# A selective-scan kernel on one core: work of the dt stage spread over other engines, and the outputs of both scan directions summed in PSUM

## Chip, core and metric

The kernel runs on one core of one Trainium2 chip. The metric is the device time of one execution in microseconds (us), lower is better. The engines are called as the profile calls them: PE (TensorE), with its weight loads apart as PEld, DVE (VectorE), ACT (ScalarE), POOL (GpSimd) and SP (SyncE, which issues all DMAs here).

## What is computed

Sixteen images of 56x56 tokens with 192 channels go through a windowed attention block with an MLP, and then through a two-dimensional selective scan:

```python
# layer 0: shifted window attention and MLP on x (16, 56, 56, 192)
...
# layer 1
xs = _cross_scan(xc)                      # rows, columns, and both reversed: K_DIRS = 4
x_dbl = jnp.einsum('bkdl,kcd->bkcl', xs, x_proj_weight)
dts, Bs, Cs = jnp.split(x_dbl, [R_RANK, R_RANK + N_STATE], axis=2)
dts = jnp.einsum('bkrl,kdr->bkdl', dts, dt_projs_weight)
dts = jax.nn.softplus(dts + dt_projs_bias[None, :, :, None])
A = -jnp.exp(A_logs).reshape(K_DIRS, d, N_STATE)
ys = _selective_scan(xs, dts, A, Bs, Cs)  # h = exp(dt*A)*h + dt*x*B ; y = sum_n h*C
ys = ys + Ds.reshape(1, K_DIRS, d, 1) * xs
y = _cross_merge(ys, h, w)                # all four directions added, the column ones transposed
y = layernorm over the channels
```

## The kernel before

The program has four parts, one behind the other, each with its own semaphores, and DRAM scratch tensors between them. Everything is float32 but where bf16 is named.

**Layer 0** (`build_layer0`) is not touched.

**The dt stage** (`build_prep`, called prep here) makes, for each image, the time steps dt, the products u = dt*x, and B and C. An image is cut into 4 chunks of 784 tokens (`CT`). A chunk has 7 items for PE (`PER`): six raw tiles of 128x784, of which tiles 0 to 2 belong to the row order (o = 0) and tiles 3 to 5 to the column order (o = 1, where `order` hands PE the tokens with a stride of 56), and a seventh with the raw B and C, called bc here. There are 16 x 4 = 64 chunks and 384 tiles. A raw tile goes into one of three PSUM slots of two banks; a fourth, `l_ps`, holds the logarithm. Softplus is computed in a form that is safe for large values:

- ACT makes r = relu(-raw - bias + 20) (L731), e = exp(20 - r) (L735) and l = log(1 + e) in PSUM (L720, `logs`). Behind the sixth tile of a chunk it copies bc to `bc_o` (L741).
- DVE makes m = e(e - 2) (L765, `quad`, one tile ahead), p = max(-m/2, l) in PSUM (L775), q = min(p, e) into `m_t` (L777), and dt = max(raw + bias, q) into `dt_o` (L788). The last reads the raw tile, so that its slot is free for PE only then (`free`, L669, waits for `dt_done`).
- POOL multiplies dt by x (L826) into `u_o`, and at the end of a chunk splits bc in one block (`split`, L797) into three bf16 parts (L805, L807, L809, L811).
- SP stores, in this order for each chunk: dt and u of o = 0, dt and u of o = 1, bc, and behind `low_done`, the end of the split, four stores of the parts (L638). At an image's first chunk the eight loads of the next image (L617, L619) stand ahead of the stores. `dt_o` and `u_o` have one buffer for each o, so L788 of tile 0 waits until the store of the chunk before has landed (`dt_out`).

**The scan** (`build_scan`) works through 16 units for each image (2 orders x 4 chunks x 2 directions d), each of 24 steps, 6144 steps in all. In a step DVE runs one scan instruction (L1071) and, in 18 of 24, one multiply (L1051) of u with B, which PE has spread over the partitions in PSUM (L951, `spread`, two steps ahead, one PSUM buffer). POOL multiplies the states by C (L1107) and makes the other six products with B (L1096). PE sums over the states (L960, `reduce`, six steps behind) into PSUM, and ACT evacuates a third of a unit at a time into `y_sb` (L1004). SP stores each unit's y to `scr_y`, which has a place for each order and direction. In column order the y's are in column order too.

**The output part** (`build_output`) loads, for each image and half of the channels (a = 0, 1), four y's and x; POOL adds the two directions of the column order (L1206), DVE those of the row order (L1228), DVE adds the columns to the rows through a transposed view (L1232) and the residual (L1237, `yf`). Then PE transposes, DVE takes statistics (L1244, L1250) and normalises (L1258) seven groups, and POOL applies weight and bias to each (L1211, L1213). POOL's queue is in order: the adds of the next image stand behind the last L1213 of this one.

The few lines that set the order in prep's end of a tile:

```python
dve.wait_ge(q_done, n + 1)
if j % 3 == 0:
    after(dve, dt_out[o], 16 * g)
    after(dve, u_done, TILES * (g - 1) + 3 * o + 3)
nc.vector.scalar_tensor_tensor(dt_o[:, o, j % 3], slot(PER * c + j), bpos[...], m, ALU.add, ALU.max)
```

## Time and profile before

| | us |
|---|---|
| median of 3 runs (lowest, highest) | 23655.29 (23637.66, 23655.61) |
| the profiled execution | 23647.01 |
| its span | 23645.2 |
| PE busy, share | 18035.3 (76%) |
| DVE busy, share | 19747.9 (84%) |
| ACT busy, share | 9462.4 (40%) |
| POOL busy, share | 16017.7 (68%) |
| mean granted TensorE clock | 0.738 |

The page draws the span in 40 equal slices, with each engine's busy share in tenths and the TensorE clock that was granted (a share of 0.50 is 1.2 GHz, 1.00 is 2.4 GHz; a figure between them is a mean over time spent at both). Layer 0 takes nine slices, prep four, the scan some 25 and the output part two. A matmul's end is modelled, so PE's busy time says less than the distance from one start to the next.

### The profile page before, as it was taken

To read this page: it belongs to the slowest core of one execution; us is meant where nothing else is said; L and a number is where in the kernel's file an instruction comes from. 1 tells how busy PE (TensorE), PEld (TensorE's weight loads), DVE (VectorE), ACT (ScalarE), POOL (GpSimd) and SP (SyncE) were. 2 spreads that over 40 slices of the span, in tenths; PEclk is the share of its full clock that TensorE was granted. 3 is DMA by queue.
4 is the path that set the end of the run, shared out by engine and by line. 5 is a ranking of instruction groups with operands and counts; after the bars stand their busy time and mean duration, and the time that the engine had idled before them with its cause. 6 is when DMAs were issued, how large, how long until landed. Compare 5 with 4: busy or idle time off the path is not lost. (4 is left out here: it accounts for less than half of the span.)

```text
span 23645.2 us, 289556 instructions
## 1 busy us (share of the span) xinstructions
PE 18035.3 (76%) x82840; PEld 6320.8 (27%) x82840; DVE 19747.9 (84%) x21684; ACT 9462.4 (40%) x14504; POOL 16017.7 (68%) x8708
## 2 busy tenths in 40 slices
PE   8999999997888677777777777777777777777711
PEld 5555565552222111111111111111111111111111
DVE  4555545446666899999999999999999999999977
ACT  3333333334444344444444444444444444444400
POOL 0000000004444899999999999999999999999956
PEclk9999999998888666666666666666666666666655
DMA  0000000004554656556655655655665565565588
GB/s 17 15 14 14 14 15 14 14 14 173 183 186 174 134 122 127 125 121 127 127 122 125 127 123 123 126 126 121 126 127 122 124 127 124 121 128 125 110 202 191
DMA packets 977931, 2571.14 MB, mean 109 GB/s; under 512 B 65622, under 2 KB 324056, under 8 KB 955296
## 3 DMA queue, kind: packets, MB, share of 16 engines
q1 hardware_dynamic: 976800, 2559.04, 47.2%
q8 instruction: 346, 5.67, 0.1%
q14 instruction: 785, 6.43, 0.1%
HBM read 1974.33 MB, written 584.45 MB: 108 GB/s over the span
## 5 line engine op out<-in xcount | busy, mean ns | idle before, releaser
L1107 POOL TENSOR_TENSOR c_pr<-c_hs,c_c_u 128x784 f32<-128x784 f32 x6144 | 11218.2, 1848 | 760.6 <-DVE c_hs L1071 760.6
L1014 ACT ACTIVATE c_psum<-c_dt_u,c_a_neg 128x784 f32<-128x784 f32 x6144 | 5642.0, 918 | 8506.9 <-DVE c_hs L1071 8462.4
L960 PE MATMUL c_psum<-c_pr,c_red 128*64 128x392 f32 x24576 | 8085.5, 779 | 0.9 <-POOL c_pr L1107 0.9
L1071 DVE TENSOR_TENSOR_SCAN c_hs<-c_psum,c_carry,c_dbx 128x784 f32<-128x784 f32 x3456 | 6273.1, 1846 | 0.0
L951 PE MATMUL c_psum<-c_br_u,c_sel 48*128 48x512 bf16 (+1 forms) x9216 | 3373.8, 461 | 3703.3 <-DVE c_dbx L1051 3626.2
L1051 DVE TENSOR_TENSOR c_dbx<-c_u_u,c_psum 128x784 f32<-128x784 f32 x4608 | 4391.4, 953 | 51.6 <-PE c_psum L951 51.6
L177 POOL TENSOR_TENSOR a_xpb<-a_x_sb,a_pb_sb 98x768 f32<-98x768 f32 x128 | 231.1, 1806 | 5070.5 <-DVE a_x L262 5057.0
L960 PEld LDWEIGHTS c_psum<-c_pr,c_red 128*64 128x64 f32 x24576 | 1924.0, 192 | 3748.4 <-issue 2031.7
L1096 POOL TENSOR_TENSOR c_dbp<-c_u_u,c_bp_u 128x784 f32<-128x784 f32 x1536 | 2849.7, 1855 | 39.8 <-DMA c_c_u<-scr_bc 39.8
L951 PEld LDWEIGHTS c_psum<-c_br_u,c_sel 48*128 48x128 bf16 x9216 | 565.3, 103 | 8504.1 <-DVE c_dbx L1051 8009.1
L1071 DVE TENSOR_TENSOR_SCAN c_hs<-c_psum,c_carry,c_dbp 128x784 f32<-128x784 f32 x1152 | 2133.5, 1852 | 0.0
L1071 DVE TENSOR_TENSOR_SCAN c_hs<-c_psum,c_dbx 128x784 f32<-128x784 f32 x1152 | 2019.4, 1782 | 19.7 <-issue 18.4
L826 POOL TENSOR_TENSOR p_u_o<-p_dt_o,p_xm 128x784 f32<-128x784 f32 x384 | 788.2, 2054 | 1276.6 <-DVE p_dt_o L788 1276.6
L689 PE MATMUL p_psum<-p_xm,p_wk 128*128 128x392 f32 x1536 | 985.6, 775 | 386.3 <-DVE p_dt_o L788 376.6
L407 PE MATMUL a_psum<-a_g_sb,a_w_sb 128*96 128x392 f32 x3072 | 1165.4, 502 | 0.7 <-ACT a_g_sb L306 0.7
L765 DVE SCALAR_TENSOR_TENSOR p_m_t<-p_e_t 128x784 f32<-128x784 f32 x384 | 459.3, 1196 | 779.5 <-ACT p_e_t L735 779.4
L213 DVE TENSOR_REDUCE a_mx<-a_psum 128x6 f32<-128x294 f32 x512 | 234.3, 458 | 1028.0 <-PE a_psum L422 1028.0
L398 PE MATMUL a_psum<-a_h2T,a_w_sb 96*128 96x392 f32 x3072 | 1044.4, 496 | 20.6 <-DVE a_v_sb L242 17.0
L1302 PE MATMUL d_psum<-d_id_sb,d_yf 96*112 96x96 f32 x896 | 152.1, 358 | 1009.2 <-DVE d_yf L1237 935.1
L436 PE MATMUL a_psum<-a_xnT,a_wqkv_sb 96*96 96x392 f32 x2048 | 747.9, 507 | 91.0 <-ACT a_qkT L336 88.6
L254 DVE COPY a_pT<-a_psum 49x384 f32<-49x384 f32 x512 | 280.5, 548 | 617.0 <-PE a_psum L471 617.0
L306 ACT ACTIVATE a_g_sb<-a_psum,a_b_sb 128x392 f32<-128x392 f32 x768 | 451.0, 587 | 765.5 <-PE a_psum L398 765.5
(105 smaller groups left out, 17490.3 us busy)
## 6 DMA issues: line engine op xcount, KB each, us to landing
c_c_u<-scr_bc SPq DMA_DIRECT2D x512, 1568.0 KB, 26.6
c_dt_u<-scr_dt SPq DMA_DIRECT2D x512, 588.0 KB, 7.3
c_u_u<-scr_u SPq DMA_DIRECT2D x512, 588.0 KB, 10.8
c_bp_u<-scr_bc SPq DMA_DIRECT2D x512, 392.0 KB, 20.2
scr_dt<-p_dt_o SPq DMA_DIRECT2D x128, 1176.0 KB, 4.5
scr_u<-p_u_o SPq DMA_DIRECT2D x128, 1176.0 KB, 5.6
scr_y<-c_y_sb SPq DMA_DIRECT2D x512, 294.0 KB, 14.4
d_yin<-scr_y SPq DMA_DIRECT2D x64, 2352.0 KB, 25.9
```

The source lines that it names most:

```text
L398: mm = pe.matmul(ps[:, 6 + m % 2, 0:UT], w1_sb[:, a, 128 * m:128 * m + 128], h2T[:, a, :], start=(a == 0), stop=(a == 1))
L407: pe.matmul(ps[0:HC, 6 + a, 0:UT], w2_sb[:, m, HC * a:HC * a + HC], g_sb[:, m, :], start=(m == 0), stop=False)
L436: mm = pe.matmul(ps[0:HC, 6 + e % 2, 0:UT], wqkv_sb[:, a, HC * e:HC * e + HC], xnT[:, a, :, 0:WT], start=(a == 0), stop=(a == 1))
L689: pe.matmul(bank(k, h), wk[:, o, 0, m0:m0 + 128], order(xm[:, par, 0, :], o, c, h, HT), start=True, stop=False)
L826: nc.gpsimd.tensor_tensor(u, dt, order(xm[:, par, k, :], o, c, 0, CT), ALU.mult).then_inc(u_done, 1)
L951: mm = pe.matmul(b_ps[:, n0:n1], sel[:, s % NPR, :], br_u[:, d, n0:n1], start=True, stop=True)
L960: mm = pe.matmul(Y(3 * w + q)[64 * h:64 * h + 64, :], red[:], pr[:, s % RP, HT * h:HT * h + HT], start=(p == 0), stop=(p == NPR - 1))
L1014: nc.scalar.activation(dA(s), dt_u[:, d, s // NPR, :], ACT.Exp, scale=a_neg[:, k, s:s + 1]).then_inc(exp_done, 1)
L1051: nc.vector.tensor_tensor(dbx[:, (MULS * w + i) % RB, :], u_u[:, d, s // NPR, :], b_ps, ALU.mult).then_inc(mul_done, 1)
L1071: nc.vector.tensor_tensor_scan(hs[:, s % RH, way], dA(s)[:, way], data, init, ALU.mult, ALU.add).then_inc(scan_done, 1)
L1096: nc.gpsimd.tensor_tensor(dbp[:, (len(POOL_STEPS) * w + i) % RG, :], u_u[:, d, s // NPR, :], bp_u[:, d, POOL_PAIRS.index(s % NPR), :], ALU ...
L1107: nc.gpsimd.tensor_tensor(pr[:, s % RP, :], hs[:, s % RH, :], c_u[:, d, s % NPR, :], ALU.mult).then_inc(prod_done, 1)
```

## The change

In **prep** ACT no longer makes relu; it copies the raw tile with the bias to SBUF (`lift` into `xb`, four buffers), which frees the PSUM slot; POOL clamps it to 20 (`clamp`); ACT takes exp (`grow`) and log (`logs`). The raw tiles have two slots in place of three, the logarithms two in place of one. ACT lifts two tiles ahead and grows one ahead. DVE computes max and min in place in PSUM and the last max from `xb`. POOL clamps two tiles ahead, multiplies by x one tile late, and does the split of a chunk in four pieces behind tiles 1 to 4 of the next chunk. SP's own order is not changed.

In the **scan** the two directions that cover a chunk are summed in PSUM: the unit that comes first ("opens") evacuates to `y_sb[:, cc]` and isn't stored; in the second, PE first multiplies `y_sb` by the identity into the PSUM group (`same`) and the reductions are added to that. Only the second is stored, half as many bytes.

In the **output part** two y's are loaded in place of four, and POOL does the one add that is left, rows plus transposed columns, in place; DVE's two adds are gone.

```diff
-    SLOT = [k % 3 for k in range(PER_IMG - 1)] + [1]
+    PER_CHUNK = TILES * PAIRS
...
-        slot = lambda k: ps[:, SLOT[k], :].rearrange("p (h z) -> p h z", h=2)[:, :, 0:HT]
-        l_ps = ps[:, 3, :].rearrange("p (h z) -> p h z", h=2)[:, :, 0:HT]
+        slot = lambda k: ps[:, k % 2, :].rearrange("p (h z) -> p h z", h=2)[:, :, 0:HT]
+        l_ps = lambda j: ps[:, 2 + j % 2, :].rearrange("p (h z) -> p h z", h=2)[:, :, 0:HT]
...
+        xb = sb("xb", [128, 4, 2, HT])
+        cap = sb("cap", [128, 2, 2, HT])
...
             def free(b, k):
...
+                img, j = (0, k - 2) if k >= 2 else (-1, k - 2 + PER_IMG)
                 if j % PER < TILES:
-                    after(pe, dt_done, TILES * (PAIRS * (b + img) + j // PER) + j % PER + 1)
+                    after(pe, xb_done, TILES * (PAIRS * (b + img) + j // PER) + j % PER + 1)
...
+            def lift(b, c, j):
...
+                act.wait_ge(raw_full, PER * g + j + 1)
+                after(act, dt_done, n - 3)
+                after(act, cap_done, n - 3)
+                nc.scalar.activation(xb[:, n_of(c, j) % 4], slot(PER * c + j), ACT.Identity,
+                                     bias=bpos[:, j // 3, j % 3:j % 3 + 1]).then_inc(xb_done, 1)
+                if j == TILES - 1:
                     act.wait_ge(raw_full, PER * g + PER)
...
                     nc.scalar.activation(bc_o[:, c % 2], slot(PER * c + TILES), ACT.Copy).then_inc(bc_done, 1)
+            def grow(b, c, j):
...
+                act.wait_ge(cap_done, n + 1)
+                after(act, q_done, n - 2)
+                nc.scalar.activation(e_t[:, j % 3], cap[:, j % 2], ACT.Exp).then_inc(e_done, 1)
+            def logs(b, c, j):
...
+                act.wait_ge(e_done, n + 1)
+                after(act, dt_done, n - 1)
+                nc.scalar.activation(l_ps(j), e_t[:, j % 3], ACT.Ln, bias=one[:, 0:1]).then_inc(l_done, 1)
+            def body(b, par, last):
+                for n in range(PER_CHUNK):
+                    for piece, ahead in ((lift, 2), (grow, 1)):
+                        at = step(b, n + ahead, last)
+                        if at:
+                            piece(*at)
+                    logs(*step(b, n, last))
...
-                        nc.vector.scalar_tensor_tensor(l_ps, m, -0.5, l_ps, ALU.mult, ALU.max).then_inc(p_done, 1)
+                        nc.vector.scalar_tensor_tensor(l, m_t[:, j % 2], -0.5, l, ALU.mult, ALU.max).then_inc(p_done, 1)
...
-                        nc.vector.tensor_tensor(m, l_ps, e_t[:, j % 3], ALU.min).then_inc(q_done, 1)
+                        nc.vector.tensor_tensor(l, l, e_t[:, j % 3], ALU.min).then_inc(q_done, 1)
...
-                        nc.vector.scalar_tensor_tensor(dt_o[:, o, j % 3], slot(PER * c + j), bpos[:, o, j % 3:j % 3 + 1], m,
-                                                       ALU.add, ALU.max).then_inc(dt_done, 1)
+                        nc.vector.tensor_tensor(dt_o[:, o, j % 3], xb[:, n_of(c, j) % 4], l, ALU.max).then_inc(dt_done, 1)
...
+            def clamp(b, c, j):
+
+                n = TILES * (PAIRS * b + c) + j
+                after(pool, e_done, n - 1)
+                hold(pool, xb_done, n + 1, fence)
+                nc.gpsimd.tensor_scalar(cap[:, j % 2], xb[:, n_of(c, j) % 4], CLAMP, None, ALU.min).then_inc(cap_done, 1)
...
+                        at = step(b, n + 2, last)
+                        if at:
+                            clamp(*at)
+                        if j >= 1:
+                            times_x(b, par, c, j - 1)
+                        elif c:
+                            times_x(b, par, c - 1, TILES - 1)
...
+                        if j in (1, 2, 3, 4):
+                            if c:
+                                split(b, c - 1, j - 1)
+                            elif not (isinstance(b, int) and b == 0):
+                                split(b - 1, PAIRS - 1, j - 1)
...
+        y_sb = sb("y_sb", [128, NCHK, 3, HT])
...
+        def opens(w):
+
+            return w % (2 * NCHK) < NCHK
...
+                if opens(w):
+                    return
                 hold(sp, y_evac, 3 * v + 3, fence)
...
                 if p == 0:
                     after(pe, y_evac, 3 * v + q - 1)
+                    if not opens(w):
+                        pe.matmul(Y(3 * w + q), same[:], y_sb[:, unit_of(w)[1], q, :], start=True, stop=False)
                 pe.wait_ge(prod_done, STEPS * v + s + 1)
...
-                                   start=(p == 0), stop=(p == NPR - 1))
+                                   start=(p == 0 and opens(w)), stop=(p == NPR - 1))
...
+                    rows = yin[:, a, 0].rearrange("p (h w) -> p h w", h=IMG)
+                    nc.gpsimd.tensor_tensor(rows, rows, yin[:, a, 1].rearrange("p (w h) -> p h w", h=IMG),
+                                            ALU.add).then_inc(add_done, 1)
...
-                    nc.vector.tensor_tensor(yin[:, a, 0], yin[:, a, 0], yin[:, a, 1], ALU.add).then_inc(row_done, 1)
...
-                    nc.vector.tensor_tensor(sq(yin[:, a, 0], "p (h w) -> p h w"), sq(yin[:, a, 0], "p (h w) -> p h w"),
-                                            sq(yin[:, a, 2], "p (w h) -> p h w"), ALU.add).then_inc(add_done, 1)
```

How the instructions move: POOL in prep, one chunk before (`p_u_o` is u, `p_parts` the bf16 parts):

```order
L826 TENSOR_TENSOR p_u_o<-p_dt_o,p_xm 128x784 x6
L805 CAST p_parts<-p_bc_o 128x784
L807 TENSOR_TENSOR p_rem<-p_bc_o,p_parts 128x784
L809 CAST p_parts<-p_rem 128x784
L811 TENSOR_TENSOR p_parts<-p_rem,p_parts 128x784
```

and the stretch of the changed kernel in which the split of a chunk is done, tiles 1 to 4 of the next chunk (`p_cap` is the clamped tile):

```order
L813 TENSOR_SCALAR p_cap<-p_xb 128x784
L825 TENSOR_TENSOR p_u_o<-p_dt_o,p_xm 128x784
L835 CAST p_parts<-p_bc_o 128x784
L813 TENSOR_SCALAR p_cap<-p_xb 128x784
L825 TENSOR_TENSOR p_u_o<-p_dt_o,p_xm 128x784
L839 TENSOR_TENSOR p_rem<-p_bc_o,p_parts 128x784
L813 TENSOR_SCALAR p_cap<-p_xb 128x784
L825 TENSOR_TENSOR p_u_o<-p_dt_o,p_xm 128x784
L842 CAST p_parts<-p_rem 128x784
L813 TENSOR_SCALAR p_cap<-p_xb 128x784
L825 TENSOR_TENSOR p_u_o<-p_dt_o,p_xm 128x784
L845 TENSOR_TENSOR p_parts<-p_rem,p_parts 128x784
```

The split's last piece now stands behind the multiplication of tile 3 of the next chunk.

DVE at the start of an image in the output part, before:

```order
L1228 TENSOR_TENSOR d_yin<-d_yin 96x3136
L1232 TENSOR_TENSOR d_yin<-d_yin 96x3136
L1237 SCALAR_TENSOR_TENSOR d_yf<-d_x_in,d_dsum,d_yin 96x3136
L1228 TENSOR_TENSOR d_yin<-d_yin 96x3136
L1232 TENSOR_TENSOR d_yin<-d_yin 96x3136
L1237 SCALAR_TENSOR_TENSOR d_yf<-d_x_in,d_dsum,d_yin 96x3136
L1244 BN_STATS d_stats<-d_psum 112x6 x4
```

and in the changed kernel:

```order
L1285 SCALAR_TENSOR_TENSOR d_yf<-d_x_in,d_dsum,d_yin 96x3136 x2
L1292 BN_STATS d_stats<-d_psum 112x6 x4
L1298 BN_AGGR d_mv<-d_stats 112x2 x4
L1292 BN_STATS d_stats<-d_psum 112x6 x4
L1298 BN_AGGR d_mv<-d_stats 112x2 x4
```

Four adds are gone from DVE; POOL's queue has two large adds for an image, as before.

## Rows read from the trace of the kernel before

**Rows 1.** Prep, scan: length; busy us of PE, PEld, DVE, ACT, POOL; PEclk, DMA share, GB/s.

```profile
5376.00:7730.00 2354.00, 1895.78 (x4120) 507.15 (x4120) 1533.78 (x1549) 1116.13 (x1217) 1126.16 (x640) 0.87 0.52 183
...
7770.00:22466.00 14696.00, 11036.03 (x33790) 2489.12 (x33790) 14669.29 (x10751) 6211.01 (x8958) 13931.45 (x7679) 0.65 0.59 124
```

**Rows 2.** Instructions of tile dt_o: ns least/median/most, first and last start.

```profile
L826 POOL TENSOR_TENSOR p_u_o<-p_dt_o,p_xm x384: 1841/2227/2593, 5404.6 to 7718.3; 128x784 f32<-128x784 f32 x192
```

**Rows 3.** Who waited for whom in prep: us in total, times, longest.

```profile
ACT p_bc_o L741 <- PE p_psum L701: 290.6, 64, 7.7
```

**Rows 4.** PE in prep in order of time: start, length, line, operands.

```profile
6210.29 3.13 PE L689 MATMUL p_psum<-p_xm,p_wk 128*128 128x392 f32 x4
...
6214.97 1.64 PE L698 MATMUL p_psum<-p_xm,p_wk 128*64 128x392 f32 x4
...
6221.25 1.58 PE L689 MATMUL p_psum<-p_xm,p_wk 128*128 128x392 f32 x4
...
6223.20 0.49 PE L691 MATMUL p_psum<-p_xm,p_wk 64*128 64x392 f32 x1
...
6227.89 2.98 PE L689 MATMUL p_psum<-p_xm,p_wk 128*128 128x392 f32 x4 [4.20 <-DVE p_dt_o L788]
```

**Rows 5.** Short stretches of the same time, columns as in rows 1.

```profile
6209.50:6211.40 1.90, 1.90 (x6) 0.51 (x3) 1.84 (x2) 0.96 (x2) 1.84 (x1) 1.00 0.42 170
...
6228.50:6230.40 1.90, 1.90 (x4) 0.67 (x2) 1.20 (x2) 0.00 (x0) 1.90 (x2) 0.50 0.77 307
```

**Rows 6.** Costliest groups, shapes apart: busy us, mean ns, idle time before and its releaser.

```profile
L765 DVE SCALAR_TENSOR_TENSOR p_m_t<-p_e_t 128x784 f32<-128x784 f32 x384 | 459.3, 1196 | 779.5 <-ACT p_e_t L735 779.4
L777 DVE TENSOR_TENSOR p_m_t<-p_psum,p_e_t 128x784 f32<-128x784 f32 x384 | 374.2, 975 | 13.1
L807 POOL TENSOR_TENSOR p_rem<-p_bc_o,p_parts 128x784 f32<-128x784 f32 x64 | 109.3, 1708 | 5.1
L805 POOL CAST p_parts<-p_bc_o 128x784 bf16<-128x784 f32 x64 | 60.3, 943 | 2.4 <-ACT p_bc_o L741 2.4
```

**Rows 7.** DVE in order of time, L765 while POOL was at work.

```profile
6234.46 1.81 DVE L765 SCALAR_TENSOR_TENSOR p_m_t<-p_e_t 128x784 f32<-128x784 f32 x1 [4.72 <-ACT p_e_t L735]
```

**Rows 8.** SP's queue at an image's first chunk: start, length, DMAs.

```profile
5988.39 1.84 SPq L638 DMA_DIRECT2D scr_bp<-p_parts  x4
...
5995.86 0.41 SPq L627 DMA_DIRECT2D scr_dt<-p_dt_o  x1
```

**Rows 9.** DMAs issued from 5990 to 6000: count, KB, median us to landing.

```profile
scr_dt<-p_dt_o SPq DMA_DIRECT2D x1, 1176.0 KB, 15.6
```

**Rows 10.** The same over all of prep.

```profile
scr_dt<-p_dt_o SPq DMA_DIRECT2D x128, 1176.0 KB, 4.5
```

**Rows 11.** All engines in the scan in order of time.

```profile
12000.48 1.57 PE L960 MATMUL c_psum<-c_pr,c_red 128*64 128x392 f32 x4
...
12005.51 0.83 PE L951 MATMUL c_psum<-c_br_u,c_sel 48*128 48x512 bf16 x2 [1.25 <-DVE c_dbx L1051]
```

**Rows 12.** POOL in the output part in order of time, first image.

```profile
22527.10 10.02 POOL L1206 TENSOR_TENSOR d_yin<-d_yin 96x3136 f32<-96x3136 f32 x1 [20.05 <-DMA d_x_in<-scr_x]
22553.23 1.80 POOL L1211 TENSOR_TENSOR d_ob<-d_ob,d_w_sb 112x768 f32<-112x768 f32 x1 [16.12 <-DVE d_ob L1258]
```

**Rows 13.** All engines, from the sixth image's last group to the seventh's first.

```profile
22925.90 4.98 POOL L1211 TENSOR_TENSOR d_ob<-d_ob,d_w_sb 112x768 f32<-112x768 f32 x1
...
22936.36 6.78 POOL L1206 TENSOR_TENSOR d_yin<-d_yin 96x3136 f32<-96x3136 f32 x1
...
22944.10 11.77 POOL L1206 TENSOR_TENSOR d_yin<-d_yin 96x3136 f32<-96x3136 f32 x1 [0.96 <-DMA d_x_in<-scr_x]
...
22962.51 5.96 DVE L1232 TENSOR_TENSOR d_yin<-d_yin 96x3136 f32<-96x3136 f32 x1
22968.51 3.48 DVE L1237 SCALAR_TENSOR_TENSOR d_yf<-d_x_in,d_dsum,d_yin 96x3136 f32<-96x3136 f32 x1
...
22978.53 1.80 POOL L1211 TENSOR_TENSOR d_ob<-d_ob,d_w_sb 112x768 f32<-112x768 f32 x1 [22.67 <-DVE d_ob L1258]
```

More of the change, by code:

```diff
@@ L795, in _, with times_x @@
         def _(pool):
-            def split(b, c):
+            def clamp(b, c, j):
+                n = TILES * (PAIRS * b + c) + j
+                after(pool, e_done, n - 1)
+                hold(pool, xb_done, n + 1, fence)
+                nc.gpsimd.tensor_scalar(cap[:, j % 2], xb[:, n_of(c, j) % 4], CLAMP, None, ALU.min).then_inc(cap_done, 1)
+            def times_x(b, par, c, j):
+                g, o, k = PAIRS * b + c, j // 3, j % 3
+                pool.wait_ge(dt_done, TILES * g + j + 1)
+                if k == 0:
+                    after(pool, u_out[o], 16 * g)
+                dt = dt_o[:, o, k].rearrange("p h t -> p (h t)")
+                u = u_o[:, o, k, :]
+                if o:
+                    dt, u = (a.rearrange("p (w r) -> p w r", r=IMG) for a in (dt, u))
+                nc.gpsimd.tensor_tensor(u, dt, order(xm[:, par, k, :], o, c, 0, CT), ALU.mult).then_inc(u_done, 1)
@@ L815, in body @@
                 for c in range(PAIRS):
[L816 removed]
                     for j in range(TILES):
[L818 to L827 removed]
+                        n = n_of(c, j)
+                        at = step(b, n + 2, last)
+                        if at:
+                            clamp(*at)
[4 more added lines that the diff above has]
+                        elif not (isinstance(b, int) and b == 0):
+                            times_x(b - 1, 1 - par, PAIRS - 1, TILES - 1)
+                        if j in (1, 2, 3, 4):
+                            if c:
+                                split(b, c - 1, j - 1)
+                            elif not (isinstance(b, int) and b == 0):
+                                split(b - 1, PAIRS - 1, j - 1)
+                if last:
+                    times_x(b, par, PAIRS - 1, TILES - 1)
+                    for part in range(4):
+                        split(b, PAIRS - 1, part)
+            clamp(0, 0, 0)
+            clamp(0, 0, 1)
             halves(pool, body)
 def build_scan(nc, io, dts, us, bcs, bps, ysc, n_img):
[L833 to L834 removed]
+    sel_h, red_h, alog_h, ident = io
+    yrow = ysc.rearrange("s a p t -> s (a p) t")
     WI = 4 * NCHK
@@ L926, in _ @@
             store(n_img - 1, WI - 1, NU - 1)
-            for d in range(2):
-                sp.wait_ge(y_out[d], 16 * NU)
+            for c in range(NCHK):
+                sp.wait_ge(y_out[c], 64 * n_img)
         def step(b, w, s):
```

150 lines of the change are left out of this document (57 added, 93 removed).

## The prediction, made before the changed kernel was run

> **What bounds the kernel now.** I read busy time by stretch first, then the waits, then each part's instructions in order of time. Layer 0 isn't touched. In the **scan** DVE is busy 14669.3 of 14696 us [rows 1]: whatever is cheaper on another engine there is worth nothing, and only a new delay of DVE counts. In **prep** no engine is full: PE 1896, DVE 1534, POOL 1126 and ACT 1116 of 2354 us [rows 1]. It is a chain with too few buffers. A raw tile holds its PSUM slot until DVE's last operation on it; at a chunk's start PE had stood still 4.20 us for that [rows 4], and ACT waits 290.6 us for bc, 4.5 us in each of the 64 chunks [rows 3]. The pace is (7718.3 - 5404.6) / 383 = 6.04 us a tile, 36.2 us a chunk [rows 2]. In the **output part** the first L1211 of image 1 starts at 22553.23 and that of image 7 at 22978.53 [rows 12, 13]: 70.9 us an image, a chain of POOL's groups, its two adds, two DVE adds and the residual.
>
> **Prep, the pace of a chunk.** With the slot freed by ACT's copy, PE can run some five tiles ahead of DVE, so I sum each engine over a chunk.
> PE: a column tile takes 6214.97 - 6210.29 = 4.68 us from start to start [rows 4] and does so at the full clock (share 1.00 from 6209.50 [rows 5]); I take 4.7. bc takes 6221.25 - 6214.97 = 6.28 us. A row tile at full clock takes 6223.20 + 0.49 - 6221.25 = 2.44 us [rows 4]. Sum: 3 x 4.7 + 6.28 + 3 x 2.44 = 27.7 us. At the low level (share 0.50 [rows 5]) the four long matmuls of a row tile take 2.98 and not 1.58 us [rows 4].
> DVE: three operations with an operand in PSUM, about 0.975 each, and `quad` at 1.196 in the mean, 1.81 with POOL at work [rows 6, 7]. So 4.1 to 4.7 us a tile, 24.7 to 28.4 a chunk.
> POOL: L826 is 1.84 at the least and 2.23 in the median [rows 2], about 2.04 over both orders; the split is 2 x 0.943 + 2 x 1.708 = 5.3 us. The clamp isn't in the trace. It has one input, like the cast at 0.943; its other bound is a two-input operation, 1.708 [rows 6]. I take 0.94, as the form is the cast's. Sum: 6 x (2.04 + 0.94) + 5.3 = 23.2 us; with the upper bound 27.8.
> ACT has about half of that to do and costs nothing but its order: behind tile 5 it waits for bc, with the next exp and log queued behind, while DVE has a tile or two in hand.
> So PE bounds a chunk at 27.7. For the ACT wait and one row tile in part at the low clock I add 1.8: **29.5 us**.
>
> **Prep, a new wait once an image.** The split's last piece now ends a chunk late, behind the product of tile 3 of the next chunk. SP waits for it in the same order as before. At an image's start that puts the part stores, the eight loads and the dt store of tiles 0 to 2 behind it: 5995.86 - 5988.39 = 7.5 us of issuing [rows 8] and then 15.6 us to landing, since the loads are ahead in the queues [rows 9]; without loads landing takes 4.5 [rows 10]. DVE needs that store landed before tile 0 of the following chunk. From dt of tile 3 the piece ends after 2.23 + 1.7 = 3.9 us, and DVE gets to the last operation of tile 0 some 3 x 4.9 - 1 = 13.7 us after it (three tiles, less that operation). The slack is 9.8; the need 7.5 + 15.6 = 23.1. DVE stands still for 13.3 us, once in each of 15 images: 200 us. The old schedule hid this, as the split ended before the next chunk began. In the other chunks the need is 1.84 + 0.4 + 4.5 = 6.7 us, under 9.8.
> Prep: 64 x (36.2 - 29.5) = 429 saved, 200 given back: **-229 us**.
>
> **Scan.** 384 identity matmuls are added, three in each of 128 closing units. They wait for an evacuation that the reduction behind them waited for anyway. One isn't in the trace; the nearest row is the reduction's group of 128x392, 1.57 us at the low clock [rows 11]. A unit lasts 24 x 14669.3 / 6144 = 57.3 us. By modelled lengths PE then has 24 x 1.57 + 18 x 0.83 + 3 x 1.57 = 57.3 us to do at the low clock, but starts lie closer than lengths, the clock's mean is 0.65 [rows 1], and nothing else waits on the extra work. I take **0**, bounds 0 and +603 (384 x 1.57). The halved y stores go behind DVE: 0; a gain is excluded but for the last store of the scan, under 10 us.
>
> **Output part.** POOL's groups of an image: seven times two operations of 1.80, with starts 1.82 apart, 25.5 us. One of them took 4.98 under DVE's L1228 [rows 13], which goes: no 3.2 any more. The transposed add on POOL isn't in the trace. L826 shows the same stride: its column form costs about 0.39 more than its row form for 784 elements [rows 2], so 6.78 + 4 x 0.39 = 8.3 us for 3136 [rows 13]. The lower bound is 6.78, the upper DVE's ratio (below). The second add meets `yf` of the first half on DVE, both from SBUF: +3.3 us, as L1211 paid against an operation of about that length. Then `yf` of the second half, 3.48, and from its end to the first L1211 22978.53 - 22971.99 = 6.5 us, as before [rows 13]. Sum: 25.5 + 8.3 + 11.6 + 3.5 + 6.5 = 55.4 us in place of 70.9. 15 periods give 232; before the first, the second half's load kept POOL waiting 20.05 us [rows 12] and is now two y's and x in place of four and x (3.6 MB of 6.0), so about 24 for both halves' loads: **-256 us**.
>
> **Sum.** -229 + 0 - 256 = -485, so the profiled execution of 23647.0 (span 23645.2) would be 23162. The median of the runs is 8 us above it: about **23170**.
>
> **A rule that speaks against the change.** The Trainium skill (GPSIMD Engine Reference, § 4.1 Engine selection) says that elementwise additions belong on VectorE, GpSimd being about twice as slow with two inputs. The contiguous case agrees by rows: POOL 6.78. What the rule would make of the transposed one is rival C.
>
> **Rivals.**
> A, *no image stall*: the loads land early enough, or DVE works the lag off. For it: PE idles then and catches up at 2.44 a tile. Against: the PE sum is the bound, so what is lost is lost. 23170 - 200 = 22970. Chance 0.15.
> B, *a chunk at 34 us*: the row tiles stay at the low clock (+3 x 1.4 and the gaps) or POOL and DVE slow each other on the shared reads of `quad` (28.4 + waits). For it: the 1.81 of rows 7. Against: PE would hardly pause. 64 x 4.5 = 288 less gained: 23460. Chance 0.13.
> C, *the transposed add is dear on POOL*: on DVE L1232 takes 5.96 [rows 13]; twice that is 11.9 us in place of 8.3. An image then takes 62.6 us, 15 x 7.2 = 108 less gained: 23280. L826 speaks against it. Chance 0.13.
> D, *PE becomes the bound of the closing units*: if PE's work at the low clock is past the 57.3 us of a unit, every identity matmul delays B for DVE: +603, so 23770, slower than before. It decides from that 57.3 on, and the sum above ties with it; against it stands that lengths overlap and part of the time is at full clock. If it comes in part only, 100 to 200 us. Chance 0.04 for all of it.
>
> **How the numbers follow.** The forecast has 0.50, A 0.15, B 0.13, C 0.13, D 0.04, and 0.05 is left for what I don't see. Changes within 0.2% (47 us) can't be told from none. A, C and the forecast with the clamp's bounds lie from 22970 to 23280; B reaches 23460. The range that leaves out D and the edge of A and B is 22940 to 23430. Only D is slower, with a little of the rest: slower 0.04, the same 0.02, faster 0.94.
>
> **What would show it.** Prep's stretch should be near 2125 us, PE's idle time small but for one gap of over 10 us an image, DVE's last max waiting for the dt store 15 times. The clamp should read about 0.9 us. The scan should keep 14670 to 14700 us, with DVE as full as now. L1260, the transposed add, should read 8.3 us in its first form and the images follow each other in 55 us. A prep above 2300 or a scan above 14800 would make the prediction wrong.

## The result, and the profile after

| | us |
|---|---|
| before, median of 4 runs (lowest, highest) | 23655.45 (23637.66, 23671.03) |
| changed, median of 4 runs (lowest, highest) | 23437.22 (23412.67, 23450.83) |
| ratio, with its 95% interval | 0.9907 (0.989 to 0.9924) |
| the profiled execution of the changed kernel | 23412.67 |
| its span | 23410.9 |

The change saves 218 us, or 0.9%. It was forecast to save 485, and the result lies 7 us outside the range. Both profiled executions are faster than their medians, by 8 and 25 us; between them lie 23647.01 - 23412.67 = 234 us, and the stretches of the changed kernel show where (columns as in [rows 1]; the lines are prep, the scan, the output part):

```profile
5376.00:7760.00 2384.00, 1801.97 (x4096) 515.90 (x4096) 1597.92 (x1546) 1014.16 (x1216) 2084.70 (x1024) 0.78 0.52 180
7804.00:22495.00 14691.00, 10765.10 (x34554) 2526.06 (x34554) 14666.12 (x10750) 6210.05 (x8958) 13940.86 (x7679) 0.70 0.57 119
22495.00:23410.00 915.00, 151.31 (x896) 133.50 (x896) 563.47 (x1378) 57.62 (x225) 665.27 (x256) 0.52 0.69 169
```

Prep is **30 us longer** than in [rows 1] (2384 against 2354), where 229 less was forecast. The scan is the same to 5 us, and with DVE as full as before (14666 of 14691). From the scan's end to the end of the span there were 23645 - 22466 = 1179 us, and now 23411 - 22495 = 916: **-263**, forecast -256. The three make -238; the passage from prep to the scan (7730 to 7770, now 7760 to 7804) is 4 us longer, which gives the 234. So one of three terms failed, prep's, and its sign of being wrong, a prep above 2300 us, is there. The column to look at there is POOL's: 2085 us busy of 2384, after 1126 of 2354. POOL's two costliest groups in the changed kernel show on what (busy us, mean ns | idle time before and its releaser):

```profile
L813 POOL TENSOR_SCALAR p_cap<-p_xb 128x784 f32<-128x784 f32 x384 | 988.7, 2575 | 139.6 <-ACT p_xb L726 106.4
L825 POOL TENSOR_TENSOR p_u_o<-p_dt_o,p_xm 128x784 f32<-128x784 f32 x384 | 786.0, 2047 | 237.8 <-DMA scr_u<-p_u_o 208.6
```

L813 is the clamp. It takes 2.58 us in the mean where the prediction took 0.94, with 1.708 as the upper bound. The waits of prep (us in total, times, longest) say who pays:

```profile
ACT p_e_t L739 <- POOL p_cap L813: 903.8, 310, 4.7
...
DVE p_psum L790 <- ACT p_psum L746: 496.6, 324, 5.3
...
DVE p_dt_o L800 <- DMA scr_dt<-p_dt_o: 223.5, 14, 16.5
...
POOL p_u_o L825 <- DMA scr_u<-p_u_o: 208.6, 17, 15.4
```

It is one chain: POOL's clamp releases ACT's exp in 310 of 384 tiles, and ACT's log releases DVE. The last two lines are another matter, the wait that the prediction named: DVE's last max stood 14 times for the store of dt, some 16 us each. In order of time, at an image's start (start us, length; SPq rows are DMAs issued):

```profile
6303.00 1.68 POOL L845 TENSOR_TENSOR p_parts<-p_rem,p_parts 128x784 bf16<-128x784 f32 x1
...
6304.91 1.84 SPq L648 DMA_DIRECT2D scr_bp<-p_parts  x4
...
6307.25 0.38 SPq L627 DMA_DIRECT2D p_xm<-scr_x  x1
...
6312.41 0.41 SPq L637 DMA_DIRECT2D scr_dt<-p_dt_o  x1
...
6328.02 0.97 DVE L800 TENSOR_TENSOR p_dt_o<-p_xb,p_psum 128x784 f32<-128x784 f32 x1 [15.54 <-DMA scr_dt<-p_dt_o]
...
6331.06 1.85 POOL L825 TENSOR_TENSOR p_u_o<-p_dt_o,p_xm 128x784 f32<-128x784 f32 x1 [14.40 <-DMA scr_u<-p_u_o]
```

The split's last piece ends at 6304.68. SP had waited for it and issues the four part stores, then the loads, and only at 6312.41 the dt store of tiles 0 to 2, 7.5 us after the part stores; it lands 15.6 us later, when DVE goes on. These are the two numbers of [rows 8, 9]. POOL stands still in the same place (14.40 us), so what should be the bottleneck loses that time too.

In the scan, the identity matmuls (L1011; ns least, median, most, then what PE idled for before them):

```profile
L1011 PE MATMUL c_psum<-c_y_sb,c_same x768: 492/627/1022, 8044.2 to 22485.3; 128*128 128x392 f32 x192
...
  issue: 220.1, 384
```

They wait for nobody and nobody is recorded as waiting for them. The output part in order of time, POOL at the first image, and then POOL and DVE at a later one:

```profile
22517.83 8.35 POOL L1260 TENSOR_TENSOR d_yin<-d_yin 96x3136 f32<-96x3136 f32 x1 [27.03 <-DMA d_x_in<-scr_x]
22533.47 8.35 POOL L1260 TENSOR_TENSOR d_yin<-d_yin 96x3136 f32<-96x3136 f32 x1 [7.29 <-DMA d_x_in<-scr_x]
22551.88 1.80 POOL L1266 TENSOR_TENSOR d_ob<-d_ob,d_w_sb 112x768 f32<-112x768 f32 x1 [10.06 <-DVE d_ob L1306]
```

```profile
23020.09 16.65 POOL L1260 TENSOR_TENSOR d_yin<-d_yin 96x3136 f32<-96x3136 f32 x2
23028.56 14.85 DVE L1285 SCALAR_TENSOR_TENSOR d_yf<-d_x_in,d_dsum,d_yin 96x3136 f32<-96x3136 f32 x2 [16.91 <-POOL d_yin L1260]
...
23049.96 1.80 POOL L1266 TENSOR_TENSOR d_ob<-d_ob,d_w_sb 112x768 f32<-112x768 f32 x1 [13.22 <-DVE d_ob L1306]
```

The transposed add on POOL takes 8.35 us, forecast 8.3. From the first L1266 of image 1 (22551.88) to that of image 10 (23049.96) there are 498.08 / 9 = 55.3 us an image, forecast 55.4. One thing is otherwise than argued: the two adds are *not* slowed (16.65 us for both). DVE's residual of the first half is; both halves take 14.85 us in place of 2 x 3.48.

### The profile page after: what moved, and what is told of

It reads as the page before. It is cut to its first block and busy times, and to the rows that moved or that the text cites. A ratio compares the mean times of both kernels' runs of the same rounds, so it can differ in the third digit from the quotient of the medians.

```text
span 23410.9 us, 290956 instructions
## 1 busy us (share of the span) xinstructions
PE 17671.3 (75%) x83608; PEld 6368.3 (27%) x83608; DVE 19513.2 (83%) x21619; ACT 9356.7 (40%) x14503; POOL 16923.9 (72%) x9092
## 5 line engine op out<-in xcount | busy, mean ns | idle before, releaser
L1014 PE MATMUL c_psum<-c_pr,c_red 128*64 128x392 f32 x24576 | 7519.3, 728 | 0.0
L1003 PE MATMUL c_psum<-c_br_u,c_sel 48*128 48x512 bf16 (+1 forms) x9216 | 3210.5, 441 | 3994.8 <-DVE c_dbx L1106 3888.7
L1106 DVE TENSOR_TENSOR c_dbx<-c_u_u,c_psum 128x784 f32<-128x784 f32 x4608 | 4390.2, 953 | 55.4 <-PE c_psum L1003 55.4
L1014 PEld LDWEIGHTS c_psum<-c_pr,c_red 128*64 128x64 f32 x24576 | 1807.9, 181 | 3522.1 <-issue 2286.9
L695 PE MATMUL p_psum<-p_xm,p_wk 128*128 128x392 f32 x1536 | 913.6, 724 | 333.7 <-ACT p_xb L726 323.6
L813 POOL TENSOR_SCALAR p_cap<-p_xb 128x784 f32<-128x784 f32 x384 | 988.7, 2575 | 139.6 <-ACT p_xb L726 106.4
L825 POOL TENSOR_TENSOR p_u_o<-p_dt_o,p_xm 128x784 f32<-128x784 f32 x384 | 786.0, 2047 | 237.8 <-DMA scr_u<-p_u_o 208.6
L790 DVE SCALAR_TENSOR_TENSOR p_psum<-p_m_t,p_psum 128x784 f32<-128x784 f32 x384 | 375.7, 978 | 509.2 <-ACT p_psum L746 496.6
```

Of the source, the lines that this page charges most:

```text
L695: pe.matmul(bank(k, h), wk[:, o, 0, m0:m0 + 128], order(xm[:, par, 0, :], o, c, h, HT), start=True, stop=False)
L813: nc.gpsimd.tensor_scalar(cap[:, j % 2], xb[:, n_of(c, j) % 4], CLAMP, None, ALU.min).then_inc(cap_done, 1)
L825: nc.gpsimd.tensor_tensor(u, dt, order(xm[:, par, k, :], o, c, 0, CT), ALU.mult).then_inc(u_done, 1)
L1003: mm = pe.matmul(b_ps[:, n0:n1], sel[:, s % NPR, :], br_u[:, d, n0:n1], start=True, stop=True)
L1014: mm = pe.matmul(Y(3 * w + q)[64 * h:64 * h + 64, :], red[:], pr[:, s % RP, HT * h:HT * h + HT], start=(p == 0 and opens(w)), stop=(p == N ...
L1106: nc.vector.tensor_tensor(dbx[:, (MULS * w + i) % RB, :], u_u[:, d, s // NPR, :], b_ps, ALU.mult).then_inc(mul_done, 1)
```

## Experiments

The theories at the start: **the clamp's price** makes POOL the bound of a chunk; against it, that **SP's order** (the wait once an image) is what eats the gain, and that **the shared reads** of `quad` and POOL slow both engines in any case. Each result but that of the eight operations is a median of four runs; its ratio is to the kernel before, measured beside it, with an interval of some 0.0017 (40 us) to either side. The medians of the kernel before were 23655.45 beside the changed kernel, 23646.34 beside the first four experiments, 23660.31 beside the next four and 23640.95 beside the last. A difference of times from two of these groups can be off by 10 to 20 us for that alone, so it is read with the ratios or with the pace. "Pace" is the distance between the first and last start of DVE's last max (384 tiles) by 383, times 6. For the changed kernel it is (7744.1 - 5399.5) / 383 = 6.12 us a tile, 36.7 a chunk. It leaves out when prep begins, and that varies: ACT's first instruction of prep starts between 5355.5 and 5386.2 us in these profiles, though layer 0 is the same in all.

### The clamp on DVE

```diff
-                nc.gpsimd.tensor_scalar(cap[:, j % 2], xb[:, n_of(c, j) % 4], CLAMP, None, ALU.min).then_inc(cap_done, 1)
+                nc.vector.tensor_scalar(cap[:, j % 2], xb[:, n_of(c, j) % 4], CLAMP, None, ALU.min).then_inc(cap_done, 1)
```

It stands ahead of the first max of each tile in DVE's order, two tiles ahead as before.

> The changed kernel with the clamp on DVE in place of POOL, and nothing else. Theory T1 (POOL bounds prep, because the clamp takes 2.58 us in the mean, in place of the 0.94 that was assumed): POOL's work on a chunk falls from 33.3 us to 6 x 2.05 + 5.0 = 17.3 us, PE at some 28 to 30 us becomes the bound, and prep falls from 2384 to 2050 to 2200 us, so the kernel to about 23150 to 23280 us. The wait of DVE for the dt store once an image stays, 14 times or so, 10 to 16 us each. Rival T2 (POOL has the most work but the stores landing late and the once-an-image wait set the pace): prep moves by less than 80 us, the kernel stays over 23350.

Measured: **23274.09** (23272.2 to 23288.65), ratio 0.9842 (0.9825 to 0.9858); pace 34.3. Two of its groups:

```profile
L787 DVE SCALAR_TENSOR_TENSOR p_m_t<-p_e_t 128x784 f32<-128x784 f32 x384 | 725.5, 1889 | 0.2 <-ACT p_e_t L739 0.2
...
L779 DVE TENSOR_SCALAR p_cap<-p_xb 128x784 f32<-128x784 f32 x384 | 223.3, 581 | 47.9 <-issue 34.4 <-ACT p_xb L726 13.5
```

163 us faster than the changed kernel, 154 by the ratios. The same operation costs 0.58 us on DVE and 2.58 on POOL. DVE no longer waits for ACT (0.2 us in all before `quad`). The expectation had PE as the next bound; but from 5900 to 6900 us DVE is busy 875 of 1000 us and PE 812, and DVE still waits for the dt store, 14 times and 194.7 us in all. So DVE is the fullest engine, not least because `quad` now takes 1.89 us in the mean.

### The clamp as a plain copy on POOL

The clamping itself is left out here; its place on the engines is kept.

```diff
-                nc.gpsimd.tensor_scalar(cap[:, j % 2], xb[:, n_of(c, j) % 4], CLAMP, None, ALU.min).then_inc(cap_done, 1)
+                nc.gpsimd.tensor_copy(cap[:, j % 2], xb[:, n_of(c, j) % 4]).then_inc(cap_done, 1)
```

> The changed kernel with POOL's clamp replaced by a plain POOL copy of the same tile; the clamping to 20 is left out, so exp is taken of the raw value. T1: the copy should take 0.85 to 1.0 us, the price that the prediction gave the clamp, POOL's work on a chunk is 23 us, and prep comes out as predicted: 2090 to 2200 us, the kernel at 23150 to 23280. If only the size of the clamp was wrong in the prediction, this kernel lands on its number. T2: prep stays within 80 us of 2384.

Measured: **23230.82** (23229.02 to 23240.59), ratio 0.9824 (0.9807 to 0.984); pace 33.7. The groups of `quad` and of the copy:

```profile
L780 DVE SCALAR_TENSOR_TENSOR p_m_t<-p_e_t 128x784 f32<-128x784 f32 x384 | 796.6, 2075 | 14.0 <-ACT p_e_t L739 14.0
...
L813 POOL COPY p_cap<-p_xb 128x784 f32<-128x784 f32 x384 | 422.5, 1100 | 117.2 <-ACT p_xb L726 113.1 <-issue 4.0
```

This is the kernel that the prediction had priced: an operation with one input, 1.10 us in the mean (the row before had 0.943). It comes to within 61 us of the forecast 23170; the changed kernel missed it by 267. So the clamp's price is the larger part of the miss. What is left over points to `quad`, 2.08 us, but this run doesn't test that.

### SP's order

The parts' stores of a chunk go behind the next chunk's stores, the next image's loads behind the first chunk's stores. The clamp stays on POOL. Two waits of SP ahead of the loads go too; they asked for the end of the image before, and the stores that now stand ahead of the loads wait for later work than that.

```diff
                 for c in range(PAIRS):
+                    store(b, c)
                     if c == 0 and not last:
-                        if not (isinstance(b, int) and b == 0):
-                            hold(sp, raw_full, PER_IMG * b, fence)
-                            hold(sp, u_done, TILES * PAIRS * b, fence)
                         load(b + 1, 1 - par)
-                    store(b, c)
+                    if c:
+                        store_parts(b, c - 1)
+                    elif not (isinstance(b, int) and b == 0):
+                        store_parts(b - 1, PAIRS - 1)
```

> The changed kernel with SP's queue in another order: the stores of B's parts of a chunk go behind the dt, u and bc stores of the next chunk, and the eight loads of the next image behind the first chunk's stores. The clamp stays on POOL. Both theories: the wait of DVE for the dt store (223.5 us) and of POOL for the u store (208.6 us) go nearly to zero. T1 (POOL bounds, and its wait adds to its work): prep falls by nearly all of POOL's 208.6 us, to about 2180 to 2200, the kernel to about 23230 to 23260. T3 (the lost time is made up anyway behind the wait, since PE and ACT run ahead): under 60 us.

Measured: **23210.18** (23195.87 to 23221.51), ratio 0.9817 (0.98 to 0.9833); pace 33.5. A short stretch, columns as in [rows 1]:

```profile
5900.00:6900.00 1000.00, 835.51 (x1904) 240.72 (x1902) 749.99 (x714) 471.52 (x565) 970.54 (x477) 0.81 0.56 198
```

227 us faster than the changed kernel by the medians, 213 by the ratios and (36.7 - 33.5) x 64 = 205 by the pace; the best that was expected was 23230. Neither DVE nor POOL waits for a store any more. What came back is nearest to POOL's own wait for the u store, 208.6 us: POOL had stood still in the same places as DVE. Now it is busy 970.5 of 1000 us, the clearest sign that POOL bounds a chunk. Its rows in this run add up to 6 x (2.577 + 2.049) + 0.843 + 1.675 + 0.837 + 1.678 = 32.8 us a chunk; the measured 33.5 holds some 0.04 us more for each of 16 starts.

### The old prep with the new scan and output part

`build_prep` is that of the kernel before, everything else that of the changed one:

```diff
-    PER_CHUNK = TILES * PAIRS
+    SLOT = [k % 3 for k in range(PER_IMG - 1)] + [1]
...
-                    after(pe, xb_done, TILES * (PAIRS * (b + img) + j // PER) + j % PER + 1)
+                    after(pe, dt_done, TILES * (PAIRS * (b + img) + j // PER) + j % PER + 1)
```

> The changed kernel with the prep part of the kernel before; scan and output part as changed. If the two halves add up: prep 2354 us as before and not 2384, the scan unchanged (14691), the output part 915, so the kernel is 30 us faster than the changed one: 23395 to 23420 us, ratio to before 0.989 to 0.990. If the changed scan had cost DVE something that the changed prep hid, it would show here as a scan over 14700 us.

Measured: **23383.95** (23375.12 to 23390.82), ratio 0.9887 (0.9871 to 0.9904). It is 53 us faster than the changed kernel, 47 by the ratios, whose intervals overlap; the expectation had 30. The traces decide: from DVE's first last max to the last there are 7724.3 - 5415.3 = 2309.0 us here and 2344.6 in the changed kernel. So, as it stands, the new prep loses time, some 36 us by this measure. The scan lasts the same with either prep (14684.7 and 14684.6 us from DVE's first scan instruction to the start of its last). The whole gain comes from the output part, which the sums in PSUM make possible. Their worth by this run is 23646.34 - 23383.95 = 262 us (the median before, beside it), forecast 256.

### Both mends together

Clamp on DVE and SP's new order, the two edits shown above in one kernel. Of POOL's part these lines go as well:

```diff
-            clamp(0, 0, 0)
-            clamp(0, 0, 1)
             halves(pool, body)
```

> The clamp on DVE (as in the first experiment) and SP's queue in the new order (as in the third). If the two costs are independent, prep falls by the sum of both: the first gave 163 us and the third 227 us under the changed kernel of 23437, so 23050 us. If POOL's or DVE's wait had only been hidden work of the other, the two would overlap: 23150 us or more.

Measured: **23077.83** (23057.4 to 23080.52), ratio 0.9754 (0.9737 to 0.977); pace 31.0. The gains of the two add up: by the ratios 0.0065 and 0.0090 make 0.0155, and 0.0153 came; by the pace 2.4 and 3.2 us a chunk, and 5.7 came. (The times alone say 163 + 227 = 390 against 359, but they are from groups whose kernel before differs by 14 us.) So each cost is there by itself, as the expectation of 23050 had it, and the rival of 23150 or more fell. The stretch, and three of its groups:

```profile
5900.00:6900.00 1000.00, 905.73 (x2058) 251.66 (x2060) 977.91 (x967) 503.04 (x611) 691.43 (x321) 0.83 0.62 217
```

```profile
L793 DVE SCALAR_TENSOR_TENSOR p_m_t<-p_e_t 128x784 f32<-128x784 f32 x384 | 736.7, 1918 | 0.2 <-ACT p_e_t L745 0.2
...
L850 POOL TENSOR_TENSOR p_rem<-p_bc_o,p_parts 128x784 f32<-128x784 f32 x64 | 153.3, 2396 | 0.1
L846 POOL CAST p_parts<-p_bc_o 128x784 bf16<-128x784 f32 x64 | 100.5, 1570 | 0.0
```

DVE is busy 978 of 1000 us, and `quad` at 1.92 is its dearest operation. POOL's side shows the same meeting: the cast takes 1.57 us and not 0.84, the subtraction 2.40 and not 1.67.

### The copy with SP's new order

The clamping is left out here too. The edit is the copy's, made on the kernel with SP's new order.

```diff
-                nc.gpsimd.tensor_scalar(cap[:, j % 2], xb[:, n_of(c, j) % 4], CLAMP, None, ALU.min).then_inc(cap_done, 1)
+                nc.gpsimd.tensor_copy(cap[:, j % 2], xb[:, n_of(c, j) % 4]).then_inc(cap_done, 1)
```

> POOL's clamp replaced by a plain POOL copy (the clamping is left out) and SP's queue in the new order. This is the prediction's kernel without both of its mis-sized terms. Theory: about 23231 - 210 = 23020 us, a chunk of 30 to 31 us, bounded no longer by POOL (23 us of work) but by DVE, whose product of e with itself takes 2.2 to 2.6 us while POOL works (both read SBUF), or by PE (28 us). If DVE is it, its idle time in prep is under 10% of the stretch; if PE, PE's start-to-start distances leave no gap in the column tiles.

Measured: **23011.88** (23001.65 to 23018.38), ratio 0.9726 (0.971 to 0.9742); pace 30.2. It is the prediction's kernel without its image stall; rival A gave 22970 for that. The stretch, and the group of `quad`:

```profile
5900.00:6900.00 1000.00, 928.34 (x2126) 248.05 (x2122) 957.68 (x797) 517.75 (x630) 864.67 (x532) 0.88 0.63 223
```

```profile
L786 DVE SCALAR_TENSOR_TENSOR p_m_t<-p_e_t 128x784 f32<-128x784 f32 x384 | 816.9, 2127 | 14.1 <-ACT p_e_t L745 14.1
```

DVE is fuller than PE here (958 against 928), where the prediction had PE at the bound, and its idle time of 4% is under the 10% that the expectation asked for. Its lengths add up to 2.127 + 3 x 0.972 = 5.04 us a tile, 30.3 a chunk, close to the pace. That sum is no proof: the same sum for the kernel with both mends, 1.918 + 0.561 + 3 x 0.971 = 5.39 us a tile, gives 32.4 a chunk against a pace of 31.0, since the recorded lengths overlap a little (in the changed kernel the `quad` of 6303.35 ends at 6305.51, and DVE's next operation starts at 6305.43). PE is close behind, and no run on this kernel separates the two; that DVE sets the pace is argued here from how full it is.

### The wait for bc, made later

ACT's copy of bc goes from behind the lift of tile 5 to behind the exp and log of the same step.

```diff
-                if j == TILES - 1:
-                    act.wait_ge(raw_full, PER * g + PER)
...
                     logs(*step(b, n, last))
+                    if n % TILES == TILES - 3:
+                        keep_bc(b, n // TILES)
```

> As the kernel with the clamp on DVE and the new order of SP, but ACT copies bc to SBUF after the exp and log of that step and not before them, so that no exp or log stands behind the wait for PE's bc. Theory that this wait costs the chunk (ACT waited for PE 145 to 159 us in 64 chunks): 40 to 120 us less than the kernel with both. Rival, that DVE or PE bounds and the wait is covered: within 20 us of it.

Measured: **23078.37** (23058.06 to 23082.98), ratio 0.9754 (0.9738 to 0.977), against 23077.83 for the same kernel without the edit. No difference in a kernel in which DVE is full (978 of 1000 us, as without the edit), so the wait is covered there. What it would cost in a kernel that PE bounds, for which the prediction's 1.8 us were meant in part, this run does not show.

### Eight operations alone on POOL

Ahead of prep, with ACT and all that hangs on it held back, POOL does eight operations of 128x784 on one source: min, max, add and mult with a constant, min and add in one instruction, a copy, and an add and a multiplication of two tensors (the same source twice). The rest is the changed kernel.

```diff
+                lambda: nc.gpsimd.tensor_scalar(t1, t0, CLAMP, None, ALU.min),
+                lambda: nc.gpsimd.tensor_scalar(t1, t0, CLAMP, None, ALU.max),
+                lambda: nc.gpsimd.tensor_scalar(t1, t0, CLAMP, None, ALU.add),
+                lambda: nc.gpsimd.tensor_scalar(t1, t0, CLAMP, None, ALU.mult),
+                lambda: nc.gpsimd.tensor_scalar(t1, t0, CLAMP, 0.0, ALU.min, ALU.add),
+                lambda: nc.gpsimd.tensor_copy(t1, t0),
+                lambda: nc.gpsimd.tensor_tensor(t1, t0, t0, ALU.add),
+                lambda: nc.gpsimd.tensor_tensor(t1, t0, t0, ALU.mult),
```

> The changed kernel with eight extra POOL operations on one tile of 128x784 float32 in SBUF, one after the other before prep's work starts, while DVE and ACT stand still: tensor_scalar with min, max, add, mult, then min followed by add; a plain copy; tensor_tensor add and mult. It costs some 20 us of time and tells why the clamp is dear. Theory P1, min is slow on POOL: min and max 2.2 us, add and mult 0.9. Theory P2, the whole form tensor_scalar is slow: all four 2.2 us, the copy 0.84, the two-input forms 1.7 to 1.85. In both, the 2.77 us that most clamps took in the changed kernel is 2.16 plus 0.6 for reads shared with DVE, and does not show here.

Measured: one run, 23411.76; POOL in order of time:

```profile
5364.32 2.17 POOL L877 TENSOR_SCALAR p_cap<-p_xb 128x784 f32<-128x784 f32 x1 [73.93 <-DVE p_one L766]
5366.57 2.17 POOL L878 TENSOR_SCALAR p_cap<-p_xb 128x784 f32<-128x784 f32 x1
5368.82 2.18 POOL L879 TENSOR_SCALAR p_cap<-p_xb 128x784 f32<-128x784 f32 x1
5371.09 2.17 POOL L880 TENSOR_SCALAR p_cap<-p_xb 128x784 f32<-128x784 f32 x1
5373.34 2.84 POOL L881 TENSOR_SCALAR p_cap<-p_xb 128x784 f32<-128x784 f32 x1
5376.24 0.84 POOL L882 COPY p_cap<-p_xb 128x784 f32<-128x784 f32 x1
5377.16 1.49 POOL L883 TENSOR_TENSOR p_cap<-p_xb 128x784 f32<-128x784 f32 x1
...
```

It is the form of the instruction and not the operation: min, max, add and mult with a constant all take 2.17 to 2.18 us, 2.6 times the copy and more than a two-tensor add (1.49, where 1.7 to 1.85 was expected; both of its inputs are the same source here); the second operation in one instruction adds 0.67. The 2.77 that is the median in the changed kernel (least 2.16) is this 2.17 and 0.6 more. Where the 0.6 comes from is in the changed kernel's rows:

```profile
6351.20 2.16 DVE L780 SCALAR_TENSOR_TENSOR p_m_t<-p_e_t 128x784 f32<-128x784 f32 x1
...
6352.62 2.77 POOL L813 TENSOR_SCALAR p_cap<-p_xb 128x784 f32<-128x784 f32 x1
...
6357.78 2.16 POOL L813 TENSOR_SCALAR p_cap<-p_xb 128x784 f32<-128x784 f32 x1
...
6358.01 1.44 DVE L780 SCALAR_TENSOR_TENSOR p_m_t<-p_e_t 128x784 f32<-128x784 f32 x1
```

The clamp at 6352.62 starts while the `quad` of 6351.20 still runs, for another 0.74 us, and takes 0.6 longer; that at 6357.78 starts first, keeps 2.16, and the `quad` behind it takes 1.44 in place of 0.97. The Trainium skill (SBUF — State Buffer, Who interferes with whom) says that a DVE instruction with two SBUF inputs contends with a GpSimd instruction that reads SBUF, and that the order of issue decides who waits. The rows agree on who pays, but not in each case on how much: the `quad` at 6358.01 has 1.93 us beside a running clamp and loses only 0.47.

### A second exp, so that `quad` reads PSUM

If `quad` is slow because both of its operands (the same `e`) come from SBUF, one of them should come from PSUM. ACT has time: it computes exp a second time, into the PSUM slot that the logarithm will overwrite. The kernel is that with both mends; ACT also works one tile further ahead, so this run changes two things.

```diff
+            def twin(b, c, j):
...
+                nc.scalar.activation(l_ps(j), cap[:, j % 2], ACT.Exp).then_inc(twin_done, 1)
...
-                    for piece, ahead in ((lift, 2), (grow, 1)):
+                    logs(*step(b, n, last))
+                    for piece, ahead in ((twin, 1), (lift, 3), (grow, 2)):
...
-                nc.vector.scalar_tensor_tensor(m_t[:, j % 2], e, -2.0, e, ALU.add, ALU.mult).then_inc(m_done, 1)
+                nc.vector.scalar_tensor_tensor(m_t[:, j % 2], l_ps(j), -2.0, e, ALU.add, ALU.mult).then_inc(m_done, 1)
```

> The kernel with the clamp on DVE and the new order of SP, in which ACT computes exp a second time into the PSUM slot that the logarithm will use, and DVE's product e(e - 2) reads one operand from there and only the other from SBUF. ACT lifts one tile and grows one tile further ahead. Theory, that DVE bounds prep because this product takes 1.92 us in place of 0.97 while POOL reads SBUF: the product takes 0.97 us every time, DVE's work falls from 5.4 to 4.5 us a tile, POOL's operations fall back to 1.67 for the split and 0.84 for the casts, PE at 28 to 29 us a chunk becomes the bound, and the kernel takes 22900 to 22960 us. Rival, that PE and the order of the copies out of PSUM already bound a chunk at 31 us: within 30 us of 23078. Rival, that the longer chain from exp over product to log costs more than it gives: over 23110.

Measured: **22906.98** (22900.66 to 22910.93), ratio **0.9688** (0.9672 to 0.9704), the fastest of all; pace (7241.6 - 5412.2) / 383 = 4.78 a tile, 28.7 a chunk. The stretch, and three groups:

```profile
5900.00:6900.00 1000.00, 962.41 (x2236) 242.46 (x2235) 863.23 (x1047) 699.66 (x872) 648.28 (x350) 0.98 0.67 236
```

```profile
L807 DVE SCALAR_TENSOR_TENSOR p_m_t<-p_psum,p_e_t 128x784 f32<-128x784 f32 x384 | 371.4, 967 | 3.5 <-ACT p_psum L753 3.3
...
L864 POOL TENSOR_TENSOR p_rem<-p_bc_o,p_parts 128x784 f32<-128x784 f32 x64 | 107.1, 1673 | 0.1
L860 POOL CAST p_parts<-p_bc_o 128x784 bf16<-128x784 f32 x64 | 53.5, 836 | 0.0
```

`quad` takes half of what it took, and POOL's split is back at its undisturbed lengths (its product with x is not, 2.29 us in both kernels). All 384 `quad`s lie between the least and the most of this row, while POOL is busy 648 of 1000 us; in the kernel with both mends they lay between 961 and 2343:

```profile
L807 DVE SCALAR_TENSOR_TENSOR p_m_t<-p_psum,p_e_t x384: 959/968/975, 5407.1 to 7236.8; 128x784 f32<-128x784 f32 x192
```

So the lengths are the operand's doing and hardly that of ACT's order. How much of the gain (0.9754 to 0.9688, 0.66% or 156 us) belongs to the order alone was not tried. Now PE is the full engine (962 of 1000), at a granted clock of 0.98, and the pace lies inside the prediction's 27.7 to 29.5 us.

## Why the prediction was wrong, and where it was right

**The clamp's price (wrong, and the main cause).** The step was "I take 0.94, as the form is the cast's", with 1.708 as its upper bound. The form is not the cast's: 2.17 us alone [eight operations], 2.58 in the mean of 384. A one-input operation was put between a one-input and a two-input row, and it lies above both. Of the 1.63 us that were missing, 1.23 are the form (2.17 alone for 0.94) and 0.4 the shared reads (2.575 for 2.17). With 2.575 the prediction's own sum for POOL is 6 x (2.04 + 2.575) + 5.3 = 33.0 us and not 23.2, past PE's 27.7; with 2.17 it is 30.6, so the form alone makes POOL the bound and the shared reads add 2.4. Prep would have been 64 x (36.2 - 33.0) = 205 saved and 200 given back, which is -5; measured +30. With the prediction's own other terms that makes -261, so 23386 for the profiled execution, where 23412.67 came. The rest is about what lies between this 33.0 and the 33.5 measured without the wait: 0.5 us a chunk, 32 us, which a sum of durations leaves out.

**The shared reads (mis-sized, second).** `quad` was put at 1.2 to 1.8 us and DVE at 28.4 at most, just above PE. With POOL nearly always at work it takes 1.9 to 2.1 in the mean. Without the image's wait the two kernels whose clamp is cured have a pace of 31.0 and 30.2 a chunk, with DVE as the fullest engine (978 and 958 of 1000 us), where 29.5 was forecast. For the first the run with the second exp shows the cause: with `quad` at 0.97 the pace is 28.7, ACT's order being the one thing changed beside it. For the second, which is nearest to the prediction's kernel, it is argued. An estimate from it: 30.2 - 29.5 = 0.7 us a chunk, 45 us, most of the 61 by which the copy missed 23170.

**PE's sum (right, but hidden).** 27.7 at full clock; 28.7 measured in the run with the second exp, where PE is the fullest engine. The 1.8 us added for ACT's wait and a low clock were not tested by themselves. In the changed kernel the mean granted clock in prep is 0.78, after 0.87 [rows 1]; PE's busy time is 1802 us, after 1896, so no row shows that this cost anything.

**The wait once an image (right).** Forecast: SP issues for 7.5 us and the store lands after 15.6, 15 times 13.3, 200 us. Seen: 7.5, 15.6, 14 times 16.0, 223.5 us; taken away by SP's order, 205 to 227 us come back. Rival A, without the wait, fell.

**The scan (right).** 0 forecast, -5 seen, and with it rival D falls. PE's 384 extra groups sit in gaps marked "issue". PE's mean granted clock in the scan is 0.70, after 0.65, and its busy time 10765 us, after 11036, so PE had more room than the sum at the low clock gave it.

**The output part (right in its numbers, one step otherwise).** 8.35 us for 8.3 and 55.3 an image for 55.4. Before the first image's groups the scan's end lies 22551.88 - 22495 = 56.9 us back, after 22553.23 - 22466 = 87.2 [rows 1, 12]: 30 us, where the prediction had about 24 without showing how. Rival C (11.9 us for the add) fell. But the second add was to pay for meeting `yf`, and it was `yf`, started later, that paid. The sum came out the same only since the total of the meeting is alike: adds 16.65, then 14.85 for both residuals, which begin 8.47 us after the adds, ends at 43.41 - 20.09 = 23.3 us, where the prediction had 8.3 + 11.6 + 3.5 = 23.4.

**Rival B** gave 34 us a chunk and 23460, the nearest number. Without the image's wait the changed kernel has 33.5. It was right by luck for the larger part. Its sum was DVE's 28.4 and waits, or row tiles at the low clock; but DVE is busy 1598 of 2384 us, and POOL sets the pace. The part of B that says that POOL and DVE slow each other is borne out, with 0.4 us a clamp or 2.4 a chunk; the form's price, which B doesn't have, is 6 x 1.23 = 7.4 a chunk on top of the 23.2.

**A page and a measurement.** The Trainium skill (GPSIMD Engine Reference, § 4.1 Engine selection) adds to the rule quoted ahead that with one input GpSimd is "roughly line-rate". For a copy a row can be read so (0.84 us for 784 elements of each partition, less than any two-input operation of that size on either engine); for an operation with a constant, which has one input too, the rows say 2.17, and the measurement decides. The part against additions holds for the contiguous one, of which the prediction gave only POOL's side, 6.78 us; DVE's is 3.41 at the least in the kernel before:

```profile
L1228 DVE TENSOR_TENSOR d_yin<-d_yin x32: 3409/3864/10030, 22500.3 to 23597.0; 96x3136 f32<-96x3136 f32 x32
```

It holds less for the transposed one: 8.35 on POOL against DVE's 5.96 [rows 13] is 1.4 times, not 2.

## What to carry to other kernels

An operation that the trace doesn't show has no upper bound in its neighbours just because it has fewer inputs: where a new operation runs once a tile on an engine that gets two other jobs with it, run it alone first, or compute at which price that engine becomes the bound (here 0.94 + (27.7 - 23.2) / 6 = 1.7 us, just the upper bound that the prediction took) and ask what rules that out. When a producer is moved later, look at every queue whose order still expects it early: here a better order on one queue was worth about as much as the whole change. And where two engines slow each other only while both are at work, as DVE's `quad` and POOL do here, a mean from a trace in which one is half idle (`quad` 1.20 us) is too small for a kernel that fills it (1.9 to 2.1).
